# Routing of the next step cut into ten parts over units 2 to 11 of a mixture-of-experts step, its combine transpose two units later

## The reference

```python
logits = x @ router_w.T                              # 16 experts
scores = sigmoid(logits);  s = scores + bias
group_score = max over pairs: top_k(s per group of 4, 2).sum()   # 4 groups
gmask = the 2 best groups;  masked = where(group picked, s, -1)
topk_idx = top_k(masked, 4)
tw = scores[topk_idx];  tw = tw / (tw.sum() + 1e-20) * 2.5
combine = one_hot(topk_idx) * tw                     # (token, expert)
h = x @ gate_w[e];  u = x @ up_w[e]
routed = sum_e combine[:, e] * ((silu(h) * u) @ down_w[e])
y = routed + (silu(x @ sh_gate) * (x @ sh_up)) @ sh_down
```

## Time and profile before

| what | value |
|---|---|
| runs | 710.6 us median (709.77 to 710.79) |
| the profiled execution's own time | 708.88 us |
| its span | 707.2 us |
| TensorE busy | 670.4 us (95%) |
| VectorE busy | 570.6 us (81%) |
| ScalarE busy | 397.7 us (56%) |
| GpSimd busy | 430.8 us (61%) |
| granted TensorE clock, mean | 0.984 of full |
| chain that ended last | PE 69%, DVE 16%, issue 8%, the DMA queue's engine 3% |

### The profile page before, as it was taken

One profiled execution on the slowest core, in us unless ns is written; L12 is line 12 of the kernel. 1 busy time (PEld: TensorE's weight loads), 2 busy tenths in 40 slices (PEclk: granted clock), 3 DMA queues, 4 the chain that ended last, 5 costly groups with the idle time before them and its releaser, 6 DMA issues.

```text
span 707.2 us, 11876 instructions
## 1 busy us (share of the span) xinstructions
PE 670.4 (95%) x3116; PEld 545.4 (77%) x3116; DVE 570.6 (81%) x1463; ACT 397.7 (56%) x784; POOL 430.8 (61%) x372
## 2 busy tenths in 40 slices
PE   4598999999999999999989999899999999999997
PEld 3386888888878877788777887678887888888885
DVE  4788887979797797987969869798698887979574
ACT  5465565565665545665446554465654565565553
POOL 4665666665666555665456565566655666666664
PEclk9699999999999999999999999999999999999999
DMA  8810542140506033051150330602406032140500
GB/s 223 299 61 21 221 137 103 72 170 2 238 2 238 3 117 125 0 187 53 57 183 0 114 125 17 238 0 73 181 15 236 5 138 117 59 197 17 239 15 16
DMA packets 30401, 76.31 MB, mean 108 GB/s; under 512 B 3584, under 2 KB 12304, under 8 KB 30352
## 3 DMA queue, kind: packets, MB, share of 16 engines
q1 hardware_dynamic: 30352, 75.79, 29.7%
HBM read 73.16 MB, written 2.62 MB: 107 GB/s over the span
## 4 chain that ended last, share of the span: by engine, by line
PE 69%; DVE 16%; issue 8%; SPq 3%; DMA 1%; DVEq 1%; ACT 1%; POOLq 0%; POOL 0%; ACTq 0%
PE gateP L411 8%; PE gateP L413 7%; PE gateP L412 7%; PE upP L411 7%; PE yP L411 7%; PE yP L413 7%; PE upP L413 7%; PE upP L412 7%; PE yP L412 7%; DVE T L951 6%; PE prepP L442 2%; DVE A L973 1%; SPq L254 1%; PE attP L457 1%; DVE ATs L920 1%
## 5 line engine op out<-in xcount | busy, mean ns | idle before, releaser
L318 POOL TENSOR_TENSOR A_lo<-A,A_hi 128x512 fp32r<-128x512 f32 x288 | 370.8, 1293 | 189.1 <-ACT A_hi L679 188.7
L662 ACT ACTIVATE gateP<-gateP 128x512 f32<-128x512 f32 x256 | 148.8, 581 | 181.6 <-PE gateP L413 180.0
L951 DVE TENSOR_TENSOR T<-gateP,CB 128x512 f32<-128x512 f32 x256 | 175.2, 684 | 63.6 <-ACT gateP L662 56.9
L679 ACT CAST A_hi<-A 128x512 fp32r<-128x512 f32 x288 | 176.8, 614 | 62.3 <-DVE A L973 58.5
L973 DVE TENSOR_TENSOR A<-upP,T 128x512 f32<-128x512 f32 x256 | 177.0, 691 | 9.2
L411 PE MATMUL gateP<-XT_hi,W_hi 128*128 128x512 f32 x288 | 124.1, 431 | 8.7 <-DVE T L951 8.3
L411 PE MATMUL upP<-XT_hi,W_hi 128*128 128x512 f32 x288 | 115.0, 399 | 2.2 <-DVE A L973 2.2
L411 PE MATMUL yP<-A_hi,W_hi 128*128 128x512 f32 x288 | 113.6, 394 | 0.6 <-POOL A_lo L318 0.6
L412 PE MATMUL gateP<-XT_hi,W_lo 128*128 128x512 f32 x288 | 114.1, 396 | 0.0
L413 PE MATMUL gateP<-XT_lo,W_hi 128*128 128x512 f32 x288 | 114.1, 396 | 0.0
L413 PE MATMUL upP<-XT_lo,W_hi 128*128 128x512 f32 x288 | 114.0, 396 | 0.0
(11 more groups left out here) (162 smaller groups left out, 642.5 us busy)
## 6 DMA issues: line engine op xcount, KB each, us to landing
CB<-combT SPq DMA_DIRECT2D x128, 512.0 KB, 6.2
out_dram<-X SPq DMA_DIRECT2D x8, 256.0 KB, 2.0
X<-in_L_attn_x_dram SPq DMA_DIRECT2D x3, 512.0 KB, 6.1
W_in<-in_L_ffn_gate_w_dram SPq DMA_DIRECT2D x4, 256.0 KB, 5.5
W_in<-in_L_ffn_up_w_dram SPq DMA_DIRECT2D x4, 256.0 KB, 5.2
W_in<-in_L_ffn_down_w_dram SPq DMA_DIRECT2D x4, 256.0 KB, 5.5
X<-in_L_attn_x_dram SPq DMA_DIRECT2D x2, 256.0 KB, 4.2
combT<-CT SPq DMA_DIRECT2D x16, 32.0 KB, 1.8
```

The lines of the kernel that those rows point to most:

```text
L318: pool.tensor_tensor(A_lo[:, slot, :], A[:, slot, :], A_hi[:, slot, :].bitcast(F32), ALU.subtract).then_inc(low_done, 1)
L662: act.activation(dst, gateP[u % 2][:, :], ACT.Silu).then_inc(silu_done, 1)
L679: act.copy(A_hi[:, v % SLOTS, :], A[:, v % SLOTS, :]).then_inc(high_done, 1)
L951: dve.tensor_tensor(T[:, u % TS, :], gateP[u % 2][:, :], CB[:, e, :], ALU.mult).then_inc(gate_weighted, 1)
```

## The change

The eight parts of `route` become ten, at w 2 to 11 (part = w - 2). The instructions and their order stay. The reciprocal becomes a part of its own, the group scores are cut after the first two instructions, the group ranks are cut between comparison and rank, the group mask goes to the part of the ranks, and the parts with the top eight, the replacement and the combine weights come two units later (w 9, 10, 11). The waits before `T` move from w 7, 8 to w 9, 10. The combine transpose goes from w 11 to w 13 and the copy to `CT` from w 12 to w 14. One wait counts one semaphore step more (base + 7 for base + 6). Step 0 gets a table that places its ten parts at w 8 to 15.

```diff
+    ROUTE_EARLY = {8: (0, 1), 9: (2,), 10: (3, 4), 11: (5,), 12: (6,), 13: (7,), 14: (8,), 15: (9,)}
...
-                        if w == (16 if early else 11):
+                        if w == (16 if early else 13):
                             transpose_weights(t0 + s + 1)
...
-                        if w == (17 if early else 12):
+                        if w == (17 if early else 14):
                             copy_weights(t0 + s + 1)
...
+                if part == 1:
                     dve.wait_ge(route_seq, base + 2)
                     dve.reciprocal(rcl[:, :, :], lg[:, :, :]).then_inc(route_seq, 1)
-                if part == 1:
+                if part == 2:          # score, sel
...
-                if part == 2:
+                if part == 3:          # hi2, pairs3[0:2]
...
-                    dve.wait_ge(route_seq, base + 6)
+                if part == 4:          # pairs3[2], gsc, ahead[0], eq
+                    dve.wait_ge(route_seq, base + 7)
...
-                if part == 3:
...
+                if part == 5:          # ahead[1], grank, gmask
...
-                if part == 4:
...
+                if part == 6:          # picked, masked
...
-                if part == 5:
+                if part == 7:          # top8
...
-                if part == 6:
+                if part == 8:          # left8
...
-                if part == 7:
+                if part == 9:          # wsel, wsum, wrec, comb
...
-                    if w in ((13, 14) if early else (7, 8)) and not (last and s == 1):
-                        dve.wait_ge(route_seq, ROUTE_OPS * (t0 + s + 1) + (16 if w in (7, 13) else 17))
+                    if w in ((13, 14) if early else (9, 10)) and not (last and s == 1):
+                        dve.wait_ge(route_seq, ROUTE_OPS * (t0 + s + 1) + (16 if w in (9, 13) else 17))
...
-                        if at + 2 <= w < at + 10:
-                            route(t0 + s + 1, w - at - 2)
+                        for part in (ROUTE_EARLY.get(w, ()) if early else (w - 2,)):
+                            route(t0 + s + 1, part)
...
-            for part in range(8):
+            for part in range(10):
```

More of the change, by code:

```diff
@@ L1012, in _ @@
             dve.wait_ge(const_seq, CONSTS)
-            for part in range(8):
-                if part in (5, 6):
-                    dve.wait_ge(route_seq, 16 if part == 5 else 17)
+            for part in range(10):
+                if part in (7, 8):
+                    dve.wait_ge(route_seq, 16 if part == 7 else 17)
                 route(0, part)
```

## The result

The changed kernel takes 728.62 us (median of four runs, 727.99 to 729.8) for 710.69 of the kernel before beside it: the ratio is 1.0255, 95% interval 1.0234 to 1.0276. It is slower, as forecast, but by 17.9 us and not 7.7. Its profiled execution has a span of 726.7 us, 19.5 more than before, so the two traces show the difference nearly whole.

The account below looks back on a forecast made before the run. TensorE, busy 95% of the span, was taken to bound the kernel. The terms 4.6 + 3.3 + 0.8 - 1.1 + 0.1 = +7.7 us on 710.6 gave 718.3 us, range 711.8 to 722.5.

Parts of the forecast that it names:

- Plain steps: Steps 1, 2, 3, 12, 13: blocked `comb` at unit 11, then statistics, delay unit 15; 0.92 us a step, +4.6 us.
- Odd steps: Attention steps 5, 7, 9, 11: combine part at unit 11 delays stage 29's `zb`; 0.8 us a step, +3.3 us.
- the bound of zero: Odd attention steps: lower bound of 0 us lost, where the overlap with GpSimd swallows all of the delay.
- Even steps 6, 8, 10: Attention steps: 0.2 us lost a step at units 11 to 13, 1.1 us won in step 6; -0.5 us in all.
- Transpose, copy, store and `CB`: Starting two units, 4.1 us, later, they still land before first use: cost nothing, or up to 1 us a step without cover.
- before any part of the routing: Unit 1 of steps with clock drops: `XT` waits there argue against the rival of a faster kernel, 706.5 us, chance 0.10.
- Even steps, units 14 and 15: Steps 4, 6, 8, 10: combine part ahead of a 0.8 us stage, then statistics; 0.2 us a step, +0.8 us.
- Step 6's gain: Step 6, unit 7: pair sums spread over units 5 and 6 remove TensorE's wait for `T`; -1.1 us.
- Step 0: Routing before the loop +0.1 us by a later third pair sum; step 0 itself 0, between -0.2 and +1.3 us.
- the clock falls more often: Rival: new waits of about a microsecond in nine steps bring TensorE clock drops of 1.5 us; four give 724, chance 0.07.

Follow-up runs that it names:

- Experiment 2: Kernel before with combine transpose and copy at units 13 and 14 and only the last of eight routing parts moved, to unit 11: 725.19 us, 1.0205.
- experiment 1: Kernel before with only the combine transpose moved to unit 13 and its copy to 14, routing still in eight parts: 716.41 us, 1.0090.
- experiment 4: Changed kernel with layernorm statistics at unit 13 instead of 12, powers at 14, normalisation at 15 and 16, except in step 0: 716.29 us, 1.0077.

## Why the prediction was right in part and wrong in size

**Plain steps: right, in place and mechanism.** The ledger named `comb` at w 11 at 1.37 us by a margin of 0.04 (0.05 in the trace), `T` of 13 starting 4.4 us behind start(13) (180.88 less 176.45), and a wait of `gateP` at unit 15. It gave 0.92 us a step for 1.09. The delay of start(15) is as forecast, 0.91 us for 0.90; of the wait, which I had put at 0.8 to 1.0, the profile counts 0.76 as idle. What was missing is the slow unit behind a wait: unit 15 takes 2.21 us and not 2.04, 0.17 more, at a granted clock of 1.00 (181.6 to 185.6). The trace of before showed it at 290.48, whose first matmul lasts 0.50 and not 0.39.

**Odd steps: right in sign, 1.18 us for 0.83, and the wrong part blamed.** I had the combine part delay stage 29. Experiment 2 puts that at 0.12 us: its wait for GpSimd takes the place of stage 29's, as the bound of zero had it. The transpose and copy alone had made these steps 0.17 longer (experiment 1). The rest, 0.9, comes with the split. Group mask, from step 5 of the changed kernel, the combine part with GpSimd's train beside it, and TensorE:

```profile
252.72 0.96 DVE L813 TENSOR_SCALAR gmask<-grank 128x16 f32<-128x16 f32 x1
...
257.91 5.03 POOL L320 TENSOR_TENSOR A_lo<-A,A_hi 128x512 fp32r<-128x512 f32 x4
...
262.07 0.90 DVE L843 TENSOR_SCALAR wsum<-wsum 128x4 f32<-128x4 f32 x1
...
263.21 0.27 DVE L848 SCALAR_TENSOR_TENSOR comb<-wsel,wrec 128x64 f32<-128x64 f32 x1
...
263.54 0.33 PE L450 MATMUL prepP<-ident,comb 128*128 128x128 f32 x1 [0.58 <-DVE comb L848]
```

`gmask` moved to w 7, met the subtraction there (0.96 us for 0.27) and made units 8 to 11 later: `A` of unit 8 starts 22.89 us into the step for 22.01 in experiment 2. VectorE's result for GpSimd's stage (`gvar`) is late with it, so GpSimd's train of four subtractions ends at 262.94, 0.87 later into the step than in experiment 2, and the combine part stands until it ends (`wsum`, over at 262.97). `comb` is then late even for a transpose two units further on, and TensorE waits 0.58 us before it also waits 0.86 for `zb`, which I had put at 1.4. I had used the mask's delay as a step in the sum but never asked whether `comb` would still make the transpose. The group mask has one tensor input. The Trainium skill (SBUF — State Buffer, in its section on SBUF's two sides) counts VectorE's two-port mode among what contends with GpSimd beside operations of two SBUF inputs. That `gmask` was blocked is shown by its 0.96 us, which end with the subtraction (253.65); that it runs in that mode is not.

**Even steps 6, 8, 10: the step that failed.** "Transpose, copy, store and `CB`. ... Cost nothing". I checked that the weights would arrive in time for their first use, and what queues behind them on SyncE. They do arrive in time. What I didn't ask is what else is slow beside traffic at the place to which they move. It is VectorE's restart behind the loop's jump, which the trace of before showed as 6.3 us for issue in two places; of what follows it I had read only the waits for `XT` ahead of the clock's falls, as something "before any part of the routing". These steps took 7.5 us more against -0.5. By units that is 8.0 in units 1 to 3, behind the restart, 2.1 in units 14 and 15, and 2.5 won in units 5 to 9. With small transfers units 1 to 3 of these steps are equal in both kernels to 0.2 us. Taking the traffic away gives 15.6 us back in the three steps, more than the change took, since the kernel before paid there too.

With the routing untouched (experiment 1) the three steps took 3.8 more, 5.3 of it in units 1 to 3. The other 2.7 us there are not the copy, which comes another 1.0 us later (38.4 us into the step for 37.4): experiment 2 has it at 37.6 and loses 8.5 there, and experiment 4 at 36.5 and loses 5.3. What goes with them is the clock: in steps 8 and 10 it is 0.83 over the first 20 us in the changed kernel and in experiment 2, and 0.91 in experiments 1 and 4. Why it stays low for longer in these two is open. I also assumed a shift of 4.1 us where it was 9.1 in the odd steps, as ScalarE's copy at unit 14 has the late `A` of unit 13 before it.

**Even steps, units 14 and 15: too small.** I took 0.2 us a step for the combine part next to the statistics; it was 0.7 in each of the four (unit 14 takes 2.69 us for 2.15, unit 15 2.19 for 2.04). In step 4 units 5 to 9 gave 0.5 back, so its +0.15 for +0.2 is luck.

**Step 6's gain: right, though this step alone does not show it.** The wait of 1.13 us at unit 7 is gone (unit 6 takes 2.40 us for 3.77), but it is gone in experiment 1 too, where the routing is untouched and step 4 has it instead. With the loop out of the way the kernel before has it in all four even steps (unit 6 takes 3.63 to 3.64), the changed one in none (2.40).

**Step 0: 1.6 for 0.1.** One of its two-input comparisons meets a subtraction (1.33 us at 50.42), and TensorE's wait for `T` grows from 0.19 to 1.01 us. Then the clock is low behind its transpose, as a window shows:

```profile
64.50:68.50 4.00, 4.00 (x15) 0.59 0.00 0
```

In the kernel before it was full there. Unit 17 of step 0 takes 4.0 to 4.1 us in every kernel with the changed step 0, and 2.8 in the others but experiment 1 (3.6). That the waits ahead bring the clock down is argued from that, not tested. Up to the end of step 0 the traces differ by up to 1.8 us with the same code (65.77 to 67.61 in six with the old step 0, 68.42 to 69.18 in five with the new one), so the 1.6 is sure only in sign.

Of the rivals, "the clock falls more often" happened and was given 0.07: the clock fell at the end of step 0, in step 5 (0.57 in the window 265.5 to 269.5) and in step 6, where it had not, and stayed low for longer in steps 8 and 10. The mean clock, 0.976 for 0.984, makes some 6 us of the 19.5, an estimate. Most of it follows the restarts, which my rival did not name; it had waits of about a microsecond in nine steps in mind, and of these only the one in step 5 brought a fall. The range ended at 722.5, since no case in it had a cost at the place where over half of the loss arises.

## What to carry to other kernels

When a transfer is moved, look at what uses the DMA engines where it lands, not only at its own deadline: an engine's restart behind a loop's jump is such a user, and it shows in a profile only as a wait for issue. Two lumps of work that each just fit need an empty unit between them. And where small instructions of one engine meet long ones of another, splitting them finer changes which of them meet: here it lost 0.9 us in the odd steps and won 0.3 to 1.7 in the even ones. An order is good for a phase, and each kind of step may want its own.

## What the hardware showed that I had not expected

VectorE's first instruction behind a loop's jump waited 1.7 us at a DMA share of 0.00, 3.1 us at 0.29 and 4.4 us at 1.02. Writing the loop out took this away at full traffic, and was worth 9.5 us to the kernel before (710.77 to 701.3).
